# Rotary preparation with the convolution of two images in three tiles; TensorE of the relative layers written out

## The reference

```python
# layers 0 and 2
attn = q*scale @ k.T + rel_h[..., :, None] + rel_w[..., None, :]
out = softmax(attn) @ v @ w_proj + b_proj
# layer 1: 7 x 7 neighbourhood and 16 register keys
scores = where(mask_cat, (q @ k_cat.T) * scale, -1e30)
out = softmax(scores) @ v_cat @ out_w.T + out_b
# layer 3: rotary positions, a mask that is added, and a depthwise convolution
v = x @ wv.T + bv
lepe = conv5x5_depthwise(v, lepe_w) + lepe_b
qr, kr = q*cos + rotate(q)*sin, k*cos + rotate(k)*sin
out = (softmax(qr @ kr.T + mask) @ v + lepe) @ wo.T + bo
```

## Time and profile before

| | us |
|---|---|
| median of 3 runs | 8723.98 |
| the profiled execution | 8719.04 |
| its span | 8717.3 |
| normalisation and `attend_rel`, layer 0 | 84.4 + 2261.0 |
| `prepare_win`, `attend_win` | 443.8 + 900.0 |
| normalisation and `attend_rel`, layer 2 | 82.9 + 2276.2 |
| `prepare_rot`, `attend_rot` | 776.3 + 1892.7 |

### The profile page before, as it was taken

The page is one execution under the profiler, slowest core; times in us unless marked ns, Lnnn a source line. Parts: engine busy times, 40 slices in busy tenths (PEclk is TensorE's granted clock), DMA queues, the critical chain, the costliest instruction groups (busy, mean ns, idle before and its releaser), DMA issues. The chain is left out here.

```text
span 8717.3 us, 168356 instructions
## 1 busy us (share of the span) xinstructions
PE 7201.7 (83%) x56896; PEld 4389.3 (50%) x56896; DVE 5013.6 (58%) x7203; ACT 3870.8 (44%) x7137; POOL 2200.3 (25%) x2407
## 2 busy tenths in 40 slices
PE   2999998999686888739999899997556599999998
PEld 1555555555354555425555555553223355555555
DVE  2655555555332666535555555553887666666666
ACT  1444444444411444404444444444111477777776
POOL 2334343434200000033434434341344000000000
PEclk7899999999876888859899999998667799999999
DMA  6666767676345655367576676754212444545453
GB/s 163 127 131 119 136 117 135 123 132 126 86 136 139 114 111 104 74 163 134 115 133 129 125 134 121 135 111 96 74 58 69 113 117 120 123 118 127 110 128 85
DMA packets 501945, 1026.90 MB, mean 118 GB/s; under 512 B 80510, under 2 KB 276768, under 8 KB 460552
## 3 DMA queue, kind: packets, MB, share of 16 engines
q1 hardware_dynamic: 453958, 931.90, 48.7%
q0 software_dynamic: 47360, 86.53, 6.2%
HBM read 658.19 MB, written 358.93 MB: 117 GB/s over the span
## 5 line engine op out<-in xcount | busy, mean ns | idle before, releaser
L1580 DVE TENSOR_REDUCE a_nmp<-a_S 128x2 f32<-128x1024 f32 x1536 | 1877.4, 1224 | 1329.9 <-PE a_S L1428 1315.1
L1681 ACT ACTIVATE a_PROB<-a_T 128x512 f32<-128x512 f32 x3072 | 1667.6, 595 | 1924.8 <-PE a_T L1407 1911.8
L1277 POOL CAST a_RF<-a_RL 32x512 fp32r<-32x512 f32 x1536 | 1295.0, 843 | 1112.5 <-DVE a_RL L1608 1020.4
L2396 DVE CUSTOM_DVE_ANT_0 a_X<-a_S,a_mask 128x1024 f32<-128x1024 f32 x768 | 910.0, 1222 | 551.8 <-PE a_S L2292 548.4
L1403 PE MATMUL a_T<-a_QW,a_KW 64*128 64x512 f32 x3072 | 812.1, 521 | 305.0 <-issue 136.9
L2437 ACT ACTIVATE a_PROB<-a_T 128x512 f32<-128x512 f32 x1536 | 835.7, 601 | 382.2 <-PE a_T L2306 382.2
L1403 PEld LDWEIGHTS a_T<-a_QW,a_KW 64*128 64x128 f32 x3072 | 313.1, 193 | 1315.5 <-issue 1312.5
L1441 PE MATMUL a_O<-a_PROB,a_V 128*32 128x512 f32 x6144 | 928.8, 680 | 2.5 <-ACT a_PROB L1681 2.5
L2306 PE MATMUL a_T<-a_ident,a_X 128*128 128x128 f32 x6144 | 824.5, 277 | 101.7 <-DVE a_OSB L2413 98.0
L2306 PEld LDWEIGHTS a_T<-a_ident,a_X 128*128 128x128 f32 x6144 | 671.6, 141 | 302.7 <-issue 284.9
L1428 PEld LDWEIGHTS a_S<-a_KV,a_QV 64*128 64x128 f32 x6144 | 658.2, 201 | 123.8
(11 more groups left out here) (182 smaller groups left out, 9399.7 us busy)
## 6 DMA issues: line engine op xcount, KB each, us to landing
a_QV<-a_part_rows SPq DMA_DIRECT2D x384, 256.0 KB, 7.1
a_rel_rows<-a_RF SPq DMA_DIRECT2D x96, 1024.0 KB, 9.2
a_K<-part_rows SPq DMA_DIRECT2D x576, 128.0 KB, 4.0
a_part_rows<-a_part SPq DMA_DIRECT2D x48, 1024.0 KB, 12.3
a_QV<-a_part_rows SPq DMA_DIRECT2D x384, 128.0 KB, 7.6
a_QV<-a_rel_rows SPq DMA_DIRECT2D x384, 128.0 KB, 6.9
a_QW<-a_rel_rows SPq DMA_DIRECT2D x192, 256.0 KB, 8.8
a_mask<-L_mask SPq DMA_DIRECT2D x48, 1024.0 KB, 7.6
```

What stands on the lines that cost most here:

```text
L1277: nc.gpsimd.tensor_copy(dst, src).then_inc(permuted, 1)
L1580: nc.vector.tensor_reduce(nmp[:, qh, c, 2 * pr:2 * pr + 2, kh], S[:, pr], AX.X, ALU.max).then_inc(s_done, 1)
L1681: nc.scalar.activation(PROB[:, s % PRING, 2 * pr + sd], T[:, slot(("st", s, pr, sd))], ACT.Exp).then_inc(t_act, 1)
L2396: nc.vector.tensor_tensor_reduce(out=X[:, v % 2, c, g], in0=S[:, sd].rearrange("p a b -> p (a b)"), in1=mask[:, n % 2, g, c], scale=1.0, s ...
```

## The change

- `prepare_rot`: the convolution works on pairs of images. Their 2 x 192 channels fill three tiles of 128 lines, with 25 taps a tile. The taps of a pair are spread over the pieces of two images: 38 (tile 0 and half of tile 1) in the pair's odd image, 37 in the image that follows; image 0 has none, and the last 37 stand at the end. Outputs "oc" of a pair (eight jobs) stand behind the "vt" jobs of the next pair's odd image. Y is double. `statistics`, `variance` and `normalise` of the next image stand behind pieces 2, 4 and 5.
- `attend_rel`, both layers: TensorE's 24 units are written out; ScalarE and VectorE keep the loop of `bodies`, SP and POOL theirs. SP's sections 1 and 2 are one written order, `opening`, with unit 1's `lines` ahead of unit 0's keys and second halves.
- `prepare_win`: the bias of v is added by VectorE as it moves T to VT; the one-row matmuls, ScalarE's copies and the line of ones fall away. VectorE waits for POOL's set-up before it begins.
- `attend_win`: SP loads near lines and operands unit by unit and the weights behind unit 0's; near lines have semaphores of their own. ScalarE copies O before the first exponential of the step.

```diff
-                            nc.tensor.matmul(T[:, to, here], XG[:, s, k, quad, P * c:P * c + P], wv[:, k],
-                                             start=k == 0, stop=False)
-                        last = nc.tensor.matmul(T[:, to, here], one_line[:], bv_line[:], start=False, stop=True)
+                            last = nc.tensor.matmul(T[:, to, here], XG[:, s, k, quad, P * c:P * c + P], wv[:, k],
+                                                    start=k == 0, stop=k == 1)
                 last.then_inc(t_ready, 1)
...
+            def values(b, j):
+                s = b % 2
+                eng.wait_ge(t_ready, done(b, ("v", j, 0), "pe"))
+                if j == 0:
+                    need(eng, v_stored[s], 16 * (b // 2))
+                alone(eng)
+                nc.vector.tensor_tensor(VT[:, s, 2 * j:2 * j + 2, :, 0:DIM],
+                                        T[:, ORDER.index(("v", j, 0)) % RING, 0:2 * CHANNELS].rearrange(
+                                            "p (c h d) -> p c h d", c=2, d=DIM),
+                                        bv[:].rearrange("p (h d) -> p h d", d=DIM).unsqueeze(1).to_broadcast(
+                                            [P, 2, HEADS, DIM]), ALU.add).then_inc(t_dve, 1)
...
             eng.wait_ge(consts_loaded, CONSTS)
+            eng.wait_ge(set_up, SETUP)
+            alone(eng)
...
                         rest(n - 1)
+                    if what == "k" and QUADS * m + at < 6:
+                        values(b, QUADS * m + at)
...
-                             ).then_inc(qk_loaded[s], 16)
+                if v >= BUFS:
+                    sp.dma_start(plain(Q_[64:66, s]), by_query[16:18].unsqueeze(1).to_broadcast([2, G, TOKENS])
+                                 ).then_inc(near_loaded[s], 16)
                 if v >= BUFS:
...
             for v in range(UNITS):
+                if v < BUFS:
+                    constants(v)
                 operands(v)
+                if v == 0:
+                    sp.dma_start(ident_sb[:], ident).then_inc(consts_loaded, 16)
+                    sp.dma_start(pick_sb[:], w["pick"]).then_inc(consts_loaded, 16)
+                    sp.dma_start(bo[:], w["bo"]).then_inc(consts_loaded, 16)
+                    for g in range(GROUPS):
+                        sp.dma_start(wo[:, g], w["wo"][g]).then_inc(consts_loaded, 16)
 
 
...
                 for s in range(STEPS):
                     t = QUADS * u + s // CHUNKS_N
-                    exponential(u, s, 0)
                     if s % CHUNKS_N == 1 and t:
                         outputs(t - 1)
+                    exponential(u, s, 0)
                     exponential(u, s, 1)
...
+            def opening():
+
+                load(0, 0)
+                lines(0, begun("qk1", 0, "dve"))
+                sp.wait_ge(t_dve, begun("v", 0, "dve"))
+                alone(sp)
+                load(0, 1)
+                store_parts(0, 0)
+                sp.wait_ge(part_stored, 16)
+                alone(sp)
+                query_rows(0, 0, 0)
+                store_tables(0, 0)
+                sp.wait_ge(rel_stored, 32)
+                alone(sp)
+                table_rows(0, 0, 0)
+                lines(1, begun("qk1", 1, "dve"))
+                sp.wait_ge(t_dve, begun("v", 1, "dve"))
+                alone(sp)
+                load(0, 2)
+                store_parts(1, 1)
+                keys(0, 0)
+                query_rows(0, 0, 1)
+                table_rows(0, 0, 1)
+                sp.wait_ge(part_stored, 32)
+                alone(sp)
+                query_rows(1, 1, 0)
+                store_tables(1, 1)
+                sp.wait_ge(rel_stored, 64)
+                alone(sp)
+                table_rows(1, 1, 0)
+                keys(1, 1)
+                query_rows(1, 1, 1)
+                table_rows(1, 1, 1)
+
             def image(hg, b, par):
                 n = hg * IMAGES + b
                 if isinstance(n, int) and n == 0:
-                    load(0, 0)
-                else:
+                    opening()
+                elif not isinstance(n, int) or n > 2:
                     section(n, par, lambda: load(hg, b))
 
             images(sp, image)
...
 
-            bodies(pe, prologue, body, epilogue)
+            prologue()
+            for u in range(UNITS):
+                body(u, u % 2)
+            epilogue()
...
+    SEQ = []
+    for _b in range(IMAGES):
+        _p, _odd = divmod(_b, 2)
+        SEQ += [("vc", _p, _j, _t) for _j in ((1, 2) if _odd else (0,)) for _t in range(2)]
+        SEQ += [(_n, _b, _g, _h) for _g in range(GROUPS) for _h in range(2) for _n in ("qk", "qkr")]
+        SEQ += [("vt", _b, _j) for _j in range(4)]
+        if _odd and _p:
+            SEQ += [("oc", _v, _m, _t) for _v in (_b - 3, _b - 2) for _m in range(2) for _t in range(2)]
+    SEQ += [("oc", _v, _m, _t) for _v in (IMAGES - 2, IMAGES - 1) for _m in range(2) for _t in range(2)]
+    AT = {n: i for i, n in enumerate(SEQ)}
 
...
+
+    HEAD_TAPS = N_TAPS // 2 + 1
+    TAPS_ODD = [(0, k) if a == 0 else (1, k) for k in range(N_TAPS) for a in range(2) if a == 0 or k < HEAD_TAPS]
+    TAPS_EVEN = [(2, k) if a == 0 else (1, HEAD_TAPS + k) for k in range(N_TAPS) for a in range(2)
+                 if a == 0 or HEAD_TAPS + k < N_TAPS]
+    TAP_AT = {n: i for i, n in enumerate(TAPS_ODD + TAPS_EVEN)}
+    PAIR_TAPS = TILES_N * N_TAPS
 
     with ExitStack() as ctx:
...
                     root(b + 1)
+                if b % 2 and b > 1:
+                    store(b - 3)
+                    store(b - 2)
+            store(IMAGES - 2)
             store(IMAGES - 1)
-            pool.wait_ge(y_stored, 16 * IMAGES)
+            for done in y_stored:
+                pool.wait_ge(done, 16 * IMAGES // 2)
 
...
+            def projected(b, m, t):
+                n, (p, odd) = ("oc", b, m, t), divmod(b, 2)
+                free(n)
+                if odd == 0 and m == 0 and t == 0:
+                    pe.wait_ge(taps, PAIR_TAPS * (p + 1))
+                alone(pe)
+                for k, (j, lines) in enumerate(((1, slice(64, P)), (2, slice(0, P))) if odd else
+                                               ((0, slice(0, P)), (1, slice(0, 64)))):
...
-            for b in range(IMAGES + 1):
-                for n in ORDER:
-                    if n[0] == "oc":
-                        if b:
-                            job(b, n)
-                    elif b < IMAGES:
-                        job(b, n)
-                    if n == ("vt", 3, 0) and b + 1 < IMAGES:
-                        mean(b + 1)
+            for b in range(IMAGES):
+                p, odd = divmod(b, 2)
+                for j in ((1, 2) if odd else (0,)):
+                    for t in range(2):
+                        padded(p, j, t)
+                for g in range(GROUPS):
+                    for h in range(2):
+                        for what in ("qk", "qkr"):
+                            rotated(what, b, g, h)
+                if b + 1 < IMAGES:
+                    mean(b + 1)
+                for j in range(4):
+                    values(b, j)
+                if odd and p:
+                    outputs(p - 1)
+            outputs(IMAGES // 2 - 1)
...
                                         ).then_inc(lo_done, 1)
+
+            def tap(p, j, k):
+                dy, dx = divmod(k, TAPS)
+                src = VP[:, p % 2, j, dy:dy + SIDE, dx:dx + SIDE]
+                dst = CV[:, p % 2, j].rearrange("p (a b) -> p a b", a=SIDE)
+                if k == 0:
+                    eng.wait_ge(t_act, TALLY[("vc", p, j, 1)])
+                    if p > 1:
+                        eng.wait_ge(t_ready, AT[("oc", 2 * p - 3, 1, 1)] + 1)
+                    alone(eng)
+                    ins = nc.vector.tensor_scalar(dst, src, lw[:, j, 0:1], lb[:, j:j + 1], ALU.mult, ALU.add)
+                else:
+                    eng.wait_ge(taps, PAIR_TAPS * p + TAP_AT[(j, k - 1)] + 1)
+                    ins = nc.vector.scalar_tensor_tensor(out=dst, in0=src, scalar=lw[:, j, k:k + 1], in1=dst,
+                                                         op0=ALU.mult, op1=ALU.add)
+                ins.then_inc(taps, 1)
 
...
             normalise(0)
             for b in range(IMAGES):
+                p, mine = (b // 2, TAPS_ODD) if b % 2 else (b // 2 - 1, TAPS_EVEN)
                 for i in range(PIECES):
                     n, (g, h) = PIECES * b + i, divmod(i, 2)
                     cols, s = slice(h * BANK, (h + 1) * BANK), n % BLOCKS
                     for src, to, bias, turn in (("qk", A, bqk, cos), ("qkr", B, bqkr, sin)):
-                        eng.wait_ge(t_ready, done(b, (src, g, h), "pe"))
+                        eng.wait_ge(t_ready, AT[(src, b, g, h)] + 1)
                         need(eng, summed, n - BLOCKS + 1)
                         alone(eng)
-                        nc.vector.scalar_tensor_tensor(out=to[:, s], in0=T[:, ORDER.index((src, g, h)) % RING],
```

(38 more changed lines are left out.)

286 lines of the change are left out of this document (132 added, 154 removed).

## The result

The changed kernel takes 8442.97 us (median of 4 runs, 8435.73 to 8455.42) against 8713.59 for the kernel before (4 runs); the ratio is 0.9694, interval 0.9635 to 0.9754. Forecast were 8460 us and a range of 8345 to 8580. The profiled execution took 8455.42 us, 263.6 less than the 8719.04 that the sum was made against, where −260 had been worked out. **The total is right and the parts are not**: two stages fell short of their forecast, and two brought far more.

A forecast was written before the change was run, and what follows sets the result against it. No single bound: barriers separate eight stages, each edit priced in its own, and prices add. −105 − 48 − 34 − 25 − 13 − 35 = −260 from 8719.0 gives 8459, said as 8460 us; 8-in-10 range 8345 to 8580.

The forecast's parts named there:

- 1, rotary preparation: Rotary preparation: 100 fewer VectorE taps and covered waits for TensorE, less new waits; −105 us (−70 to −130).
- the turn of an image: Rotary preparation: VectorE's new wait for the next image's first products, 9.9 us an image on average (6 to 12).
- 2, TensorE written out: Relative layers: without its loop TensorE's second transposed scores start 2.65 us earlier at 18 jumps; −48 us (−22 to −171).
- The low clock after the gap stays: Relative layers: TensorE's low clock behind each jump's standstill was taken as unchanged by writing TensorE out.
- Rival B: Relative layers: ScalarE's return gates everything, so writing TensorE out gives 0 in place of −48, total 8507 us; chance 0.10.
- Rival A: Relative layers: ScalarE returns quickly alone, so the whole jump goes; −171 in place of −48, total 8337 us; chance 0.12.
- 3, the opening: Both relative layers: unit 1's lines issued earlier shorten TensorE's opening standstill, 17 us a layer; −34 us (−21 to −39).
- 4, window preparation: Window preparation: removing 192 one-row bias matmuls shortens the chain 3.5 us an image; −25 us (−8 to −42).
- 5, the start of the window attention: Window attention: TensorE starts earlier with only unit 0's loads ahead, less 7 us for later units; −13 us (0 to −20).
- 6, ScalarE's copy: Window attention: copying outputs before the first exponential saves 0.47 us at each of 90 waits; −35 us (0 to −50).
- The slower rival: Relative layers: TensorE's written-out stream of 40 units stands for its own code, total 9139 us; chance 0.03.

The follow-up runs named there:

- the short sum: POOL's sum of A and B cut to 8 of 512 columns in the rotary preparation, against the changed kernel: 8410.71 us.
- the fastest kernel: TensorE's jobs at an image's turn reordered, against the changed kernel with ScalarE written out and rotary products of pieces 1-2 and 3-4 paired: 8253.98 us.
- those of zeros: 192 one-row matmuls of zeros put back in the window preparation, bias still added by VectorE, against the changed kernel: 8530.82 us.

## Why the prediction was right in the sum and wrong in its parts

**1, rotary preparation: −105 forecast, −66.** The step that failed is "After the change POOL's sum A+B is called in each piece just as VectorE begins 7.5 us of taps, so I let it run only in the next piece's two products (1.5 us)". The exclusion is real, but the sum, which comes between the low part and the first tap, gets in first, and the tap waits 1.0 us, 42 times: 42 us, where the forecast had 3.7 x 7 = 26 us of waiting for sums (measured 0.6) and 7 us for n_rstd (2.9). The Trainium skill (SBUF — State Buffer, "SBUF: two separate sides") says that whichever of the two starts first gets the ports for its whole instruction; the 2.28 us rows agree, and so does the row of the short sum. The forecast took the rule and asked only who had waited before. The second part: the turn of an image cost 12.7 us on average over images 2 to 7 (counted from 0) and not 9.9, 8.6 to 16.4, and image 1's 20.3; the fastest kernel shows it to be TensorE's order of jobs. So of the 15.8 us an image that were taken off as covered, 12.7 came back at the turn. The 120 us for 100 fewer taps were right: 473.1 to 406.6 us of VectorE is 66.5, and 42 for the sums and 0.12 for each tap that directly follows its own tile's, some 10 us, make it up. (The forecast took 0.13 for that; the two numbers that it named, 1.275 and 1.20, give 0.075. The 0.13 was a guess that came out.)

**2, TensorE written out: −48 forecast, nothing measured.** The forecast's reading of the jump was right: ScalarE's return binds, and TensorE's second pair of transposed scores comes 2.71 us a jump earlier, where 2.65 had been worked out. The step that failed is "The low clock after the gap stays". The gap was only moved and partly filled, so that TensorE runs more of the following jobs at the low clock (143 us in place of 90), and the extra step itself waits 14.2 us for ScalarE; two steps on, the gain is gone. The longer waits for QC, 23 us, were put at nothing too. Rival B has the right size, 0, but its reason (ScalarE's return gates everything) is not what happened. Rival A is out: ScalarE's return takes as long without TensorE's beside it.

**3, the opening: −34 forecast.** The standstill shortened by 20 us in each layer, a little above the upper end of 10.7 to 19.3 that the forecast gave. The stages themselves can't confirm the size: with TensorE's loop kept, one profile has layer 0 shorter by 2.0 us and layer 2 by 42.9.

**4, window preparation: −25 forecast, −99.5.** The term was mis-sized twice. A pair of a k and a v job fell from 3.99 to 2.59 us at the full clock: 1.40, of which the two one-row matmuls are 1.04 from start to start and the rest is that the jobs next to them got shorter too. The forecast had about 1.3, but for three of an image's six v jobs; an image is 12.4 us shorter on average, more than all six give. And the clock was low for 14 to 34 us of an image, mostly 31, where it now is for 10. The forecast took off "some for TensorE's clock"; it was to be added.

**5, the start of the window attention: −13 forecast, 17 to 33 us measured.** The start is 21.7 us earlier, as in the sum. With the new place of the copy it is worth 33 us, with the old one 17 (902 to 884), one profile each; whether the 7 us set against it for the later units were lost is not settled by these.

**6, ScalarE's copy: −35 forecast, −81 measured, −65 with the old loads (902 to 836).** The waits are 43 us less, as reckoned (42). About as much again came from TensorE's clock.

So 39 and 65 us that did not come in 1 to 3 were met by 75 and 35 more than forecast in 4 to 6. That the total hit within 17 us of the median is luck in the sizes. The slower rival (the written-out stream starves TensorE) did not occur: with ScalarE written out too, the same stream gives the shortest stages of all.

## What to carry to other kernels

Where TensorE sets the pace, price a wait or a weak job on its path at more than its own length: here 43 us of short waits cost 81, 71 us of one-row matmuls 99.5, and 99.5 us of standstills at the jumps 131, for the granted clock was low in part of the work behind them. A standstill that is only moved gave nothing. A loop's return has to be taken out of every engine that TensorE waits for within a step: out of one engine it gave 0 or 33 us here, out of both 106. And look at what the faster engine then waits for: here the transfers of QC. Put what VectorE does with two SBUF inputs where POOL has nothing to do, and jobs that feed the next image's first product ahead of those that feed nothing soon.

## What the runs showed of the hardware that was not expected

- POOL's sum (1.53 us on average) and a two-input tap on VectorE exclude each other in both directions: before, a POOL operation of 0.71 us lasted 34.19 under back-to-back taps; after, a tap of 1.28 lasts 2.28 behind a sum already begun.
- One-row matmuls lengthen their neighbours: at the full clock the eight v matmuls of a job take 1.59 us with them and 1.30 without. With those of zeros the stage has 197 us at the low clock against 119 without.
- A loop's back jump keeps ScalarE away for 5.4 to 9.5 us (mean 8.0) when TensorE jumps with it and 5.6 to 9.1 (mean 7.8) when not, in the kernels before and after. The same jump on VectorE takes 0.3.
- A tap that follows the one whose result it adds to starts 1.32 us behind it; with another between, 1.20. A tap over 128 partitions lasts 1.28 us, as over 96.
- At like standstills a different part of the low clock falls on work: at the jump at 767 us before, 6.0 of 10.2 us at the low clock lay behind the standstill of 7.19 us; at the one at 750 us after, 9.2 of 13.7 behind one of 6.63.
